# Expert attention of an audio tower: another order of the fills, copies and row steps, and values weighed ahead of the maxima on TensorE

## The reference

```python
sx = jnp.einsum('bsd,ndh->bnsd', x, hl_w) + hl_b[None, :, None, :]
pad = sx == 0
q = jnp.einsum('bnsd,neod->bneso', sx, wq)
k = jnp.einsum('bnsd,nod->bnso', sx, wk)
v = jnp.einsum('bnsd,nod->bnso', sx, wv)
scores = jnp.einsum('bnesd,bntd->bnest', q, k) * d ** 0.5 + causal
att = jax.nn.softmax(scores, axis=-1)
qkv = jnp.einsum('bnest,bntd->bnesd', att, v)
qkv = jnp.where(pad[:, :, None], 0.0, qkv)
...
gs = jax.nn.softmax(jnp.einsum('bnsf,nef->bnse', out, gate_w) + gate_b[None, :, None, :], axis=-1)
mixed = jnp.einsum('bnsed,bnse->bnsd', out.reshape(b, nh, s, ne, d), gs)
hn = layernorm(mixed + resid, ln_g, ln_b)
...
hx = jnp.where(pm, 0.0, fx @ fc1_w.T + fc1_b)
hx = jax.nn.relu(hx)
hx = jnp.where(pm, 0.0, hx @ fc2_w.T + fc2_b)
hx = layernorm(hx + fx, fnorm_g, fnorm_b)
fg = jax.nn.softmax(fout @ fgate_w.T, axis=-1)
```

## Time and profile before

| | us |
|---|---|
| median of 3 runs | 2044.35 |
| the 3 runs | 2043.14, 2044.35, 2044.68 |
| profiled execution, its own time | 2043.27 |
| its span in the trace | 2041.3 |
| of the span, expert attention | some 858 (555 to 1413) |
| busy in the whole span: PE, DVE, ACT, POOL | 1713.3, 1350.3, 775.0, 602.4 |

### The profile page before, as it was taken

One profiled execution on the slowest core, in us unless ns is written; L12 is line 12 of the kernel. 1 busy time (PEld: TensorE's weight loads), 2 busy tenths in 40 slices (PEclk: granted clock), 3 DMA queues, 4 the chain that ended last, 5 costly groups with the idle time before them and its releaser, 6 DMA issues. The chain is left out here.

```text
span 2041.3 us, 45282 instructions
## 1 busy us (share of the span) xinstructions
PE 1713.3 (84%) x15237; PEld 1253.0 (61%) x15240; DVE 1350.3 (66%) x4295; ACT 775.0 (38%) x2210; POOL 602.4 (30%) x906
## 2 busy tenths in 40 slices
PE   1499999999669988888888888872899999788887
PEld 1266666666535555555555555551788888677776
DVE  6276666666526666666666666664766666588887
ACT  2254445454234444444444444420222222343443
POOL 2522222222134333333333333333211112222221
PEclk9999999999789887777777777775555555688988
DMA  2000000000000000000000000000000000000000
GB/s 112 1 2 0 0 0 0 0 0 0 1 1 1 2 1 0 0 0 0 0 0 0 0 0 0 0 1 0 1 0 0 0 0 1 1 5 5 6 4 13
DMA packets 6979, 8.13 MB, mean 4 GB/s; under 512 B 6272, under 2 KB 6272, under 8 KB 6784
## 3 DMA queue, kind: packets, MB, share of 16 engines
q1 hardware_dynamic: 6912, 7.25, 1.0%
HBM read 5.71 MB, written 1.54 MB: 4 GB/s over the span
## 5 line engine op out<-in xcount | busy, mean ns | idle before, releaser
L962 POOL TENSOR_SCALAR_AFFINE_SELECT ex_pT<-ex_pT 128x512 f32<-128x512 f32 (+1 forms) x256 | 135.7, 554 | 315.0 <-ACT ex_pT L1176 272.9
L604 ACT ACTIVATE al_prob<-al_S,al_negmax 94x94 f32<-94x94 f32 (+1 forms) x512 | 146.2, 376 | 180.0 <-DVE al_negmax L731 180.0
L505 PE MATMUL al_S<-al_kpad,al_qT 128*94 128x376 f32 x384 | 166.4, 516 | 0.0
L682 POOL TENSOR_TENSOR al_kpad<-al_kT,al_quad_mask 128x1504 f32<-128x1504 f32 x32 | 86.2, 2694 | 186.2 <-ACTq L619 186.2
L731 DVE TENSOR_REDUCE al_negmax<-al_S 94x2 f32<-94x376 f32 (+1 forms) x192 | 99.2, 542 | 62.6 <-PE al_S L506 56.7
L1599 POOL TENSOR_TENSOR ta_kk<-ta_ext 94x320 f32<-94x320 f32 x64 | 60.4, 962 | 246.2 <-DVE ta_qkn L1779 161.6
L1250 DVE TENSOR_REDUCE ex_negmaxA<-ex_R 128x4 bf16<-128x512 f32 x128 | 89.1, 696 | 56.9 <-PE ex_R L1028 51.4
L971 POOL TENSOR_TENSOR ex_zrstd<-ex_zvar,neg_half 94x16 f32<-94x16 f32 x34 | 98.6, 2900 | 28.9 <-DVE ex_zvar L1329 28.9
L741 DVE RECIPROCAL al_rec<-al_O 128x188 f32<-128x188 f32 x64 | 84.9, 1327 | 32.1 <-PE al_O L543 32.1
L1169 ACT ACTIVATE ex_pT<-ex_T 128x496 f32<-128x496 f32 x128 | 74.8, 584 | 76.0 <-PE ex_T L1066 76.0
L1176 ACT ACTIVATE ex_pT<-ex_T 128x496 f32<-128x496 f32 x128 | 74.8, 584 | 73.8 <-PE ex_T L1045 73.7
(11 more groups left out here) (321 smaller groups left out, 4413.3 us busy)
## 6 DMA issues: line engine op xcount, KB each, us to landing
tok_xin<-x_t SPq DMA_DIRECT2D x4, 760.0 KB, 7.3
wsb<-weights SPq DMA_DIRECT2D x1, 2531.0 KB, 14.0
out<-stream SPq DMA_DIRECT2D x16, 94.0 KB
tok_par<-tok_w SPq DMA_DIRECT2D x1, 4.5 KB, 1.7
```

The costliest lines, as they stand in the source:

```text
L505: nc.tensor.matmul(S[0:P, k, 0:2 * N], q, s, start=True, stop=False)
L604: last = nc.scalar.activation(p[:, k, cols], S[0:P, k, cols], ACT.Exp, bias=negmax[g % 2][:, m:m + 1])
L682: nc.gpsimd.tensor_tensor(kpad[par][:].rearrange("p j g n -> p j (g n)"), kT[:].rearrange("p g n -> p (g n)").unsqueeze(1).broadcast_to([1 ...
L962: nc.gpsimd.affine_select(out=view, in_=view, compare_op=ALU.is_ge, fill=0.0, base=shift, pattern=[[0, NH], [1, cols]], channel_multiplier ...
```

## The change

Only `expert_attention` is changed. The arithmetic is the same; the steps move:

- TensorE: `weigh` of a unit stands ahead of `max_scores` of the unit two ahead. The fill `xT` moves from U0 of the next body (where it stood first) to U3 of the body in which its row is normalised, behind `weigh`; its place in `FILLS` is now between `v` and `fc2`. The fill `fg` stands ahead of `weigh`, `kb01`, `v` and `pickA` keep their unit, and most fills stand at another place in it. In U2 `pickB` stands ahead of `queries`, and in U3 `q23` does.
- ScalarE: the queries are copied ahead of the exponentials of heads 0 and 1, so that the semaphore `tA_exp` and its two waits go; the copies stand in the order of the fills; `fexp` moves from U2 to U1, and the exponential of the gate ahead of the copy of `xT` in U3.
- GpSimd: the tail steps of a unit (`rstds`, `zrstd`, `mixed`) stand ahead of the causal masks, and `rstds` moves to U1.
- VectorE: the read of `fc2` moves from the head of the next body to the end of this one. The read of `fg` moves up, ahead of the residual additions. The layer norm's output `xn` moves up to stand ahead of `pickB`; `maxima(rf, 0)` and `mask_values(ru, 1)` move ahead of the gate's sums; the last gate's chain (`fsum` to the addition to `stream`) moves from ahead of `maxima(rf, 1)` to behind `mask_values(ru, 2)`. A small tile `ftop` takes the place of a part of `top`.

The diff, cut to its core:

```diff
 
-        FILLS = [("xT", FRONT), ("znT", MLP), ("fg", LAST), ("sx", FRONT),
+        FILLS = [("znT", MLP), ("fg", LAST), ("sx", FRONT),
                  ("pickA", TAIL), ("kb01", FRONT), ("kb23", FRONT), ("q01", FRONT),
                  ("pickB", TAIL), ("fc1", MLP), ("k", FRONT),
-                 ("q23", FRONT), ("v", FRONT), ("fc2", MLP)]
+                 ("q23", FRONT), ("v", FRONT), ("xT", LN), ("fc2", MLP)]
         PER_ROW = {"sx": 2, "v": 2}
 
...
                                 .then_inc(sem["mixed_ready"], 1)
+                    r = t - UNIT
+                    if valid(r):
+                        p = pT[e % 2]
+                        pool.wait_ge(sem["tB_used"], r * NE + e + 1)
+                        pool.wait_ge(sem["tA_used"], r * NE + e + 1)
+                        pool.sem_inc(sem["settled"], 1)
+                        for first, cols, shift in ((0, K0, 0), (N, K1, QB)):
...
-                    pe.wait_ge(sem["tA_used"], u + 1)
+                    need(pe, sem["tA_used"], u)
                 else:
...
@@ -1097,44 +1098,44 @@
                         if not valid(nr):
                             first.then_inc(sem["tA_full"], 1)
                         scores(ru, par, e, (2, 3)).then_inc(sem["tB_full"], 1)
-                    if e == 0 and valid(rf):
-                        pe.wait_ge(sem["xn_ready"], rf + 1)
-                        fill(t, "xT", by_halves(C, P, lambda h: xn[:, h, :], lambda h: ident[0:P, 0:P]))
-                    if e == 1 and valid(rt):
-                        pe.wait_ge(sem["o_used"], NE * (rt + 1))
-                        fill(t, "pickA", picks(odd, slice(0, P)))
-
-                    if valid(nr):
-                        queries(nr, npar, ne).then_inc(sem["tA_full"], 1)
                     if e == 0 and valid2(rm):
                         pe.wait_ge(sem["zn_ready"], rm + 1)
                         fill(t, "znT", by_halves(128, P, lambda h: zn[odd][:, h].rearrange("p a c -> p (a c)"),
                                                  lambda h: ident[0:P, 0:P]))
-                    if e == 1 and valid(rf):
-                        pe.wait_ge(sem["sx_used"], 2 * (rf + 1))
-                        fill(t, "kb01", padded_keys((0, 1)))
+                    if e == 1 and valid(rt):
+                        pe.wait_ge(sem["o_used"], NE * (rt + 1))
+                        fill(t, "pickA", picks(odd, slice(0, P)))
                     if e == 2 and valid(rt):
                         fill(t, "pickB", picks(odd, slice(P, N)))
                     if e == 3 and valid(rf):
                         fill(t, "q23", projections((2, 3)))
 
-                    if valid(fr):
-                        max_scores(fr, fpar, fe)
+                    if valid(nr):
+                        queries(nr, npar, ne).then_inc(sem["tA_full"], 1)
                     if e == 0 and valid(rl):
                         fill(t, "fg", by_halves(P, NH, lambda h: znT[odd][:, h * P:(h + 1) * P], lambda h: w("fgate")))
+                    if e == 1 and valid(rf):
+                        pe.wait_ge(sem["sx_used"], 2 * (rf + 1))
+                        fill(t, "kb01", padded_keys((0, 1)))
+                    if e == 3 and valid(rf):
+                        fill(t, "v", [(X[:, 0:C], sxT[odd][:, 0:K0], w("ewv")),
+                                      (X[:, C:2 * C], sxT[odd][:, QB:NP], w("ewv"))])
+
+                    if e == 0 and valid(rt):
+                        weigh(rt, odd, 3)
+                    if e > 0 and valid(ru):
+                        weigh(ru, par, e - 1)
                     if e == 1 and valid(rf):
                         fill(t, "kb23", padded_keys((2, 3)))
                     if e == 2 and valid(rm):
                         pe.wait_ge(sem["znT_used"], rm + 1)
                         fill(t, "fc1", [(X[:, 0:N], w("fc1"), znT[odd][:])])
-                    if e == 3 and valid(rf):
-                        fill(t, "v", [(X[:, 0:C], sxT[odd][:, 0:K0], w("ewv")),
-                                      (X[:, C:2 * C], sxT[odd][:, QB:NP], w("ewv"))])
-
-                    if e == 0 and valid(rt):
-                        weigh(rt, odd, 3)
-                    if e > 0 and valid(ru):
-                        weigh(ru, par, e - 1)
+                    if e == 3 and valid(t):
+                        pe.wait_ge(sem["xn_ready"], t + 1)
+                        fill(t, "xT", by_halves(C, P, lambda h: xn[:, h, :], lambda h: ident[0:P, 0:P]))
+
+                    if valid(fr):
+                        max_scores(fr, fpar, fe)
                     if e == 0 and valid(rf):
                         pe.wait_ge(sem["xT_used"], rf + 1)
                         fill(t, "sx", [(X[:, 0:N], w("hl_t", C), xT[:])])
...
-                    if valid(ru):
-                        act.wait_ge(sem["tA_full"], u + 2)
-                        ins = nc.scalar.activation(pT[e % 2][:, 0:2, :], T[:, 0:2, 0:PAIR], ACT.Exp)
-                        ins.then_inc(sem["tA_exp"], 1)
-                        if not valid(nr):
-                            act.wait_ge(sem["tA_exp"], u + 1)
-                            act.sem_inc(sem["tA_used"], 1)
-                    if valid(nr):
-                        if not valid(ru):
-                            act.wait_ge(sem["tA_full"], 1)
-                        nc.scalar.activation(qm[ne % 2][:], T[:, 0, QCOL:QCOL + N], ACT.Copy).then_inc(sem["m_used"], 1)
-                        act.wait_ge(sem["m_used"], nr * NE + ne + 1)
...
+                    if valid(nr):
+                        act.wait_ge(sem["tA_full"], nr * NE + ne + 1)
+                        nc.scalar.activation(qm[ne % 2][:], T[:, 0, QCOL:QCOL + N], ACT.Copy).then_inc(sem["m_used"], 1)
...
+                    if valid(ru):
+                        if not valid(nr):
+                            act.wait_ge(sem["tA_full"], u + 2)
+                        nc.scalar.activation(pT[e % 2][:, 0:2, :], T[:, 0:2, 0:PAIR], ACT.Exp).then_inc(sem["tA_used"], 1)
...
+                    if e == 3 and valid(rt):
+                        act.wait_ge(sem["gate_ready"], rt + 1)
+                        nc.scalar.activation(gate_exp[:], gate[:], ACT.Exp).then_inc(sem["gexp_ready"], 1)
+                    if e == 3 and valid(t):
+                        act.wait_ge(sem["xT_full"], t + 1)
+                        used("xT_used", xT[:], slice(0, C), slice(0, N))
...
-                if valid(rn):
-                    dve.wait_ge(sem["fc2_full"], rn + 1)
-                    tt(hx[:], X[0:P, 0:HALVES * C].rearrange("p (h c) -> p h c", h=HALVES), over_halves("fc2_b"), ALU.add)\
-                        .then_inc(sem["fc2_used"], 1)
...
+                if valid(rl):
+                    dve.wait_ge(sem["fg_full"], rl + 1)
+                    gates = X[0:P, 0:HALVES * NH].rearrange("p (h n) -> p h n", h=HALVES)
...
+                if valid(t):
+                    dve.wait_ge(sem["rstd_ready"], t + 1)
+                    need(dve, sem["xT_full"], t)
+                    for h in range(HALVES):
+                        last = ts(xn[:, h, :], stream[:, t * HALVES + h, :], moments[:, h, 0:1], rstd[:, h:h + 1],
+                                  ALU.subtract, ALU.mult)
+                    last.then_inc(sem["xn_ready"], 1)
                 if valid(rt):
                     pick_heads(rt, 1, "pickB")
+                if valid(rf):
+                    maxima(rf, 0)
+                if valid(ru):
+                    mask_values(ru, 1, par)
+                if valid(rt):
                     dve.wait_ge(sem["pickB_used"], rt + 1)
                     flat = gate[:].rearrange("p h n f -> p h (n f)")
...
+                if valid(rf):
+                    maxima(rf, 1)
+                if valid(rt):
+                    dve.wait_ge(sem["gexp_ready"], rt + 1)
+                    flat = gate_exp[:].rearrange("p h n e -> p (h n) e")
+                    link(red(top[:], flat, AX.X, ALU.add))
+                    link(nc.vector.reciprocal(top[:], top[:]))
+                    tt(gate[:].rearrange("p h n e -> p (h n) e"), flat,
+                       top[:].unsqueeze(2).broadcast_to([P, HALVES * NH, NE]), ALU.mult).then_inc(sem["gs_ready"], 1)
+                if valid(ru):
+                    mask_values(ru, 2, par)
                 if valid(rl):
                     dve.wait_ge(sem["fexp_ready"], rl + 1)
...
+                if valid(rm):
+                    dve.wait_ge(sem["fc2_full"], rm + 1)
+                    tt(hx[:], X[0:P, 0:HALVES * C].rearrange("p (h c) -> p h c", h=HALVES), over_halves("fc2_b"), ALU.add)\
+                        .then_inc(sem["fc2_used"], 1)
```

More of the change, by code:

```diff
@@ L831, in expert_attention @@
         top = sb("top", [P, HALVES * NH])
+        ftop = sb("ftop", [P, HALVES])
         gate_exp = sb("gate_exp", [P, HALVES, NH, NE])
@@ L980, in body @@
                                 .then_inc(sem["mixed_ready"], 1)
+                    r = t - UNIT
[5 more added lines that the diff above has]
```

(18 more changed lines are left out.)

81 lines of the change are left out of this document (19 added, 62 removed).

## The result

The changed kernel took 2108.22 us (median of 4 runs, 2107.72 to 2112.52), the kernel before 2044.31 beside it (4 runs): a ratio of 1.0318, 95% interval 1.0300 to 1.0336. The forecast was 2052 in a range of 2012 to 2081. The profiled execution took 2112.52 with a span of 2110.6, 69.3 more than the span before.

A forecast was written before the change was run, and what follows sets the result against it. TensorE's work (89% busy, clock 0.77) and waits were taken to bound the kernel. Slots +0.8 and clock -0.4 gave +0.4 us a row, +11 over 27 rows, less 3 at the start: +8, 2052 us, range 2012 to 2081.

The forecast's parts named there:

- the term of the clock: Steady rows: products behind which the clock rises come 1.7 us earlier, so 1.7 us less half clock, -0.4 us a row.
- the start: First rows of the stage, without `fc2` or last gate: `xT` and `fg` go out of the way, 5 rows by 0.6, -3 us.
- The order at an equal clock: Sum of the four slot terms over a row, clock unchanged: -1.7 + 0.6 + 0.6 + 1.3 = +0.8 us.
- (b): U2: `fc1` starts at 3.4 us, with `k` and `max_scores` behind it; U2 takes 5.4 us instead of 4.84, +0.6.
- (c): U3: `v` starts at 2.0 us, `xT` and `max_scores` follow; U3 takes 5.2 us instead of 4.66, +0.6.
- (d): Boundary: VectorE's queue delays the read of `fc2`; the wait passes to `znT`, from 1.0 to some 2.3 us, +1.3 a row.
- (a): U0 and U1: `xT`'s 0.82 us slot leaves and the 0.88 us wait for `fg` goes, together -1.7 us a row.
- the last gate's chain 1.56: VectorE's queue at the boundary: the moved chain was counted at its earlier length, 1.56 us, ahead of the read of `fc2`.
- The price of 0.24 us: Cost of each us at half clock, from two rows: 1.59 us longer for 6.6 us more half clock.
- The clock did not come back at once: Faster rival: clock returns early in U0, row 23.8 to 24.9 us, likeliest 2011 us; 0.37 shared with slot terms too large.
- The rival on the slow side: Clock falls in U3 already, behind waits in U2 and U3: row 26.8 to 27.2 us, time 2081; chance 0.13.
- the marks: Profile signs: `znT` waits 2.3 us, no `sx` wait for `fg`, TensorE idle over 3.5 us a row, clock 0.76 to 0.82.

The follow-up runs named there:

- b1: Kernel before with 5 spare 128x512 products ahead of the fill `xT` and 5 ahead of `sx`: 1972.6 us, ratio 0.966.
- a9: Changed kernel with 13 spare 128x512 products ahead of `znT` and 4 ahead of `pickA`: 2005.8 us, ratio 0.983.
- a7: Changed kernel with GpSimd's causal masks put ahead of the tail steps again, as before the change: 2092.8 us, ratio 1.024.
- a8: Changed kernel with weighing put behind `max_scores` again in U3 alone: 2064.9 us, ratio 1.011.
- a3: Changed kernel with 15 of 16 components of GpSimd's product `mixed` left out: 2094.4 us, ratio 1.026.

## Why the prediction was wrong

The direction was right, and so was the hand-over of the boundary's wait to `znT`; the size was not: +64 us against +8. In the profiled execution, +69, the steady rows cost 29 us more than forecast (22 x (1.72 - 0.4)), the start 20, and the first four rows 12. Two steps failed: the term of the clock, which had the wrong sign, and the start, which had no term for it.

- **The order at an equal clock, +0.8 us a row.** The sum was nearly right, and in part by luck. Between rows at full clock it is 23.58 - 22.56 = +1.0, or up to 0.3 more, since b1's spare products end some 0.3 us behind the read of `fc2` and a9's end with it. The terms inside it were off in both directions. U2 took 4.98 and U3 5.07 us, not 5.4 and 5.2: (b) and (c) were too large by 0.4 and 0.1. `v` came 1.87 us behind `scores` (2.0 forecast) and `fc1` waited 0.48 us. (d) was too small: `znT` came 3.86 us behind `scores` and not 3.1, and waited 2.93 and not 2.3. Term (a) can only be read together with (d) and the clock: U0 and U1 took 17.26 us on average (16.00 before), +1.26, where the three made -0.8. At full clock, with the spare products in, they took 13.52 in a9 and 12.94 in b1, and U2 and U3 together 10.02 and 9.62. So the +1.0 is +0.6 in the first half and +0.4 in the second, where I had -0.4 and +1.2. The step "the last gate's chain 1.56" of (d) failed: from `fsum` (1086.95) to the read of `fc2` (1089.30) it took 2.35 us beside GpSimd. I had the chain behind the gate's product, which lets `mixed` start, at its length from before, and I had "cost at nothing" the moves on GpSimd, of which the tail steps ahead of the masks are 0.58 of the 0.91 us (a7).
- **The clock, -0.4 us a row.** This failed, and in its sign. I let the half clock begin at the boundary and end by where the products stand that follow, so that fewer slots meant less half clock. It is 13.65 us in every row, where it had been 11.8 (0.46 of 25.59). It costs the changed kernel 27.31 - 23.58 = 3.73 us a row, and before 25.59 - 22.56 = 3.03: +0.7, not -0.4. The price of 0.24 us that I read from two rows was right (3.73 / 13.65 = 0.27, and 3.03 / 11.8 = 0.26). What the two rows could not tell is what sets the length, and I took it from the work, not from the wait which I had just made three times as long. By the Trainium skill (TensorE: Matmul & The Clock Gate, section "HAM oscillation — how this bites in real kernels") idle gaps of TensorE set off the half clock, there in a kernel that waits for a transfer in each tile. b1 fits this for the waits of the kernel before (0.99 and 0.88 us; filled, the clock went from 0.77 to 0.99). Its price of half the length is not borne out in the steady rows (0.27).
- **The first four rows.** I took the same +0.4 for them as for the steady ones. They had had a clock of 0.89 and 24.0 us, and this is gone: +3.3 us each.
- **The start, -3 us.** It was +16.6. I took `xT` and `fg` out of slots and had no term for the clock. Slower work on TensorE is 15.0 of the 16.6 us: the mean clock is 0.75 over 124.74 us where it was 0.86 over 108.11, which makes some 32 us more at half clock (2 x (0.25 x 124.74 - 0.14 x 108.11)). That is 0.47 us for each, more than the 0.27 of the steady rows. A stretch of 13.65 us of it begins at 586.9. Undoing U3's order gives all of it back (a8), but a short `mixed` gives back 11.9 (a3), and the clock is high in both. The windows up to the first read in a3, a8 and a9:

```profile
555.00:667.86 112.86, 81.61 (x880) 49.21 (x881) 49.32 (x153) 42.35 (x106) 37.30 (x84) 0.87 0.01 1
```

```profile
555.00:660.80 105.80, 78.72 (x867) 48.11 (x869) 49.15 (x151) 42.09 (x105) 38.23 (x81) 0.89 0.01 1
```

```profile
555.00:674.56 119.56, 94.11 (x941) 56.16 (x952) 48.38 (x151) 42.34 (x106) 37.83 (x82) 0.89 0.01 1
```

a9 has the clock of a8 there and still reads `fc2` first at 674.56; its spare products take 15 us more of TensorE's time there (22.99 against 7.91 in the helper's line), in a stretch that has no wait for `fc2` yet. So a9 does not speak against the clock. What makes the clock fall at 586.9 stays open: a3 has the same steps and the same waits on TensorE up to there (1.04, 0.51 and 0.65 us), and its clock did not fall.
- **The rivals.** The clock did not come back at once. The rival on the slow side (2081, a row of up to 27.2) had nearly the right row with the wrong place: U3 ran at full clock. Of the marks, the waits and the idle time (4.0 us) came true in kind, and the clock of 0.75 lay just below the 0.76 to 0.82 expected. The range ended at 2081 because that rival stood on the same kind of clock argument and had no term for the start.
